# Moving key norms, the gated output, the second head's turn and two down-weight rotations inside one attention phase's hand-written engine orders

## The chip, the cores and the metric

The kernel runs on one core of a Trainium2 chip. It is one program with one launch. The metric is device time in microseconds (us), from the first to the last instruction and what lies around them; lower is better. Five engines run their own instruction lists side by side and meet only at semaphores: TensorE (PE: matmuls and transposes, which write PSUM), VectorE (DVE), ScalarE (ACT), GpSimd (POOL) and SyncE (SP, which issues the DMAs here).

## The reference, cut to what matters

Four stages work on x (16 x 112 x 512) with a context of 16 x 375 x 512: a causal cross attention, a feed forward stage with Hadamard transforms, a second cross attention with projected and normalized keys, and a last attention. The change lies in the first. That phase also prepares work for later stages: the keys and values of the third stage, which need only the context, and the turned and rotated weights of the second.

```python
x = x + tanh(g_xattn[0]) * L0_xattn(layernorm(x), ctx, ctx)      # first attention: q = layernorm(x), k = v = ctx
#   scores = q k^T / sqrt(32), causal mask, softmax, 16 heads of 32
x = x + tanh(g_ffn[0]) * L0_ffn(layernorm(x))                    # fwht, W_up and W_gate, silu, fwht, W_down
x = x + tanh(g_xattn[1]) * L1_xattn(layernorm(x), ctx)           # k = rms_norm(ctx @ Wk), v = ctx @ Wv, 4 heads of 128
x = x + tanh(g_ffn[1]) * L1_ffn(layernorm(x))
```

## The kernel before, in words

`phase_a` holds the first attention, and runs from about 6 us to about 688 us of the span. It works through B = 16 batches. Each has 8 pairs of heads (`PAIRS`, n = 0 to 7). PE, DVE and ACT each have a loop over b and n in which `if n == ...` lines set, by hand, at which place of that engine's list a step stands. An engine takes its list in this order, and a step that waits holds all that stand behind it. The names `cur`, `before` and `after` say that batch b, b - 1 or b + 1 exists.

The attention part of a pair: PE makes the scores of four heads (`scores`, for every second n), DVE masks and takes the maxima of a pair (`maximum(b, n)`), ACT takes the exponentials (`exps(b, n)`), PE turns the two heads' probabilities one after the other through one PSUM tile (`turn_probs(b, n, 0)`, then `(b, n, 1)`). After the first, ACT copies the tile out (`probs_copy`, semaphore `pT_first`); PE may fill the tile again only then. After the second, DVE copies (`pT_second`), and the first turn of the next pair waits for that. `weigh` multiplies by the context for a group of two pairs. After the batch `turn_back` turns the output, and DVE scales it (`gated`, semaphore `tmp_done`); POOL adds it to x (`residual`).

Beside this, in each batch:

- The context of the next batch is turned in three chunks (`turn_ctx(b + 1, c)`), and split in two float32r parts by ACT (`ctx_hi`) and DVE (`ctx_lo`). `turn_ctx(b + 1, 2)` writes the bank of the value projection, so PE waits there until ACT has copied the values of chunk 0 (`values_out(b, 0)`, semaphore `v_out`).
- The keys and values of the third stage are projected in three chunks, each in two halves of six matmuls (`project(b, "k" or "v", c, half)`). When the keys of a chunk stand in their bank, ACT squares them (`square_keys`), DVE sums the squares (`sum_keys`), POOL adds an epsilon and takes the power -1/2 (`key_norms`, tile `a_rk`), and DVE scales the keys (`scale_keys`, tile `a_kn`, semaphore `kn_done`). `project(b, "k", c + 1, 0)` writes the same bank, so PE waits for `kn_done`; `turn_keys` turns the scaled keys.
- Jobs for the second stage's weights (`run_job`, at n = 1, 3, 5, 7) turn gate, up and down weights through the bank `outp`, which many steps share: each waits for the reader of the use before (`free_out`). Down weights are first rotated on POOL (`rotate_down(b, 0 to 3)`, in batches with b % 4 of 0 or 1); the first job of b % 4 = 2 waits for all eight of these.
- DVE takes the moments of the next x (`moments(b + 1)`), POOL its deviation (`deviations`), DVE normalizes it (`normalize`, tile `a_xn`).

Of pair 1 to pair 3 the orders are, with the semaphore of a step's own waits left out. DVE, n = 1: `ctx_lo(b + 1, 0)`, `gated(b - 1)`, `probs_copy(b, 1)`, `moments(b + 1)`; n = 2: `maximum(b, 4)`, `sum_keys(b, 0)`, `probs_copy(b, 2)`, `maximum(b, 5)`, `normalize(b + 1)`; n = 3: `scale_keys(b, 0)`, `ctx_lo(b + 1, 1)`, `ctx_lo(b + 1, 2)`, `probs_copy(b, 3)`. ACT, n = 2: `square_keys(b, 0)`, `probs_copy(b, 2)`, `copy_out`, `exps(b, 4)`, `values_out(b, 0)`, `ctx_hi(b + 1, 1)`. POOL, per batch: `residual(b - 1)`, `deviations(b + 1)`, `key_norms(b, 0)` and what the diff shows.

Before the loop come the first turns and splits, and the split of the two projection weights into two parts (`weights_hi(0)`, `weights_hi(1)` on ACT, 2048 elements a row each; `weights_lo` on DVE).

## Time and profile before

| what | value |
|---|---|
| median of 3 runs | 2236.51 us (2234.78 to 2236.95) |
| profiled execution | 2239.38 us, its span 2237.7 us, mean granted TensorE clock 0.965 |
| busy over the span | PE 92%, DVE 59%, ACT 51%, POOL 30% |
| phase of the first attention | about 6 to 688 us |

The profiled execution stands 2.9 us above the median. Rows of the timeline give the start in us from the span's start, the duration in us, the engine, the line of the code, the tile written and the tiles read, how many instructions are merged, and in brackets the idle time of the engine ahead of the row and what ended it. A clock of 1.00 is TensorE's upper level of 2.4 GHz, 0.50 is the lower of 1.2 GHz.

### The profile page before, as it was taken

The page shows a single profiled execution, that of the slowest core. Times are in us where ns is not written, and L with a number is a line of the kernel's source. Part 1 is how long each engine was busy: PE and PEld are TensorE (multiplying, and loading weights), DVE is VectorE, ACT ScalarE, POOL GpSimd, SP SyncE. Part 2 cuts the span into 40 slices and gives each one's busy share as a digit, 9 for nine tenths or more (in the row PEclk, how much of TensorE's full clock was granted, in tenths as well). Part 3 has the DMA queues.
Part 4 walks back from the last instruction along what each step waited for, and adds up shares of the span by engine and source line. Part 5 has one row for each costly group of instructions (what it writes and reads, how often), then busy time and mean ns, then how long its engine had stood idle before and what let it go on. Part 6 is the DMA issues. An engine that isn't in the chain of part 4 may idle for free. (4 is left out here: it accounts for less than half of the span.)

```text
span 2237.7 us, 38580 instructions
## 1 busy us (share of the span) xinstructions
PE 2068.8 (92%) x13464; PEld 1704.7 (76%) x13464; DVE 1319.6 (59%) x2603; ACT 1148.4 (51%) x3025; POOL 664.6 (30%) x814
## 2 busy tenths in 40 slices
PE   5999999999998999999978996999999999689997
PEld 4767777777766888888857884888888888578884
DVE  5665656656654454465436554777777776466664
ACT  4555656556553333354323443766776676245542
POOL 1333523523522000000003442555555555012221
PEclk9999999999999999999989998999999999889997
DMA  4333534534328320010013344332223221221010
GB/s 147 122 115 123 150 90 133 183 90 139 113 70 301 103 73 18 1 66 29 1 67 107 114 125 133 102 105 94 74 92 104 96 80 37 78 73 47 26 34 26
DMA packets 167398, 205.96 MB, mean 92 GB/s; under 512 B 63680, under 2 KB 105664, under 8 KB 166752
## 3 DMA queue, kind: packets, MB, share of 16 engines
q1 hardware_dynamic: 167264, 204.15, 28.9%
q8 instruction: 87, 1.43, 0.3%
q14 instruction: 47, 0.39, 0.0%
HBM read 128.13 MB, written 75.99 MB: 91 GB/s over the span
## 5 line engine op out<-in xcount | busy, mean ns | idle before, releaser
L1730 POOL TENSOR_TENSOR c_probs<-c_probs,c_rsum 112x375 f32<-112x375 f32 x256 | 212.8, 834 | 231.5 <-DVE c_rsum L1840 225.6
L1836 DVE TENSOR_REDUCE c_nmax<-c_score 112x1 f32<-112x375 f32 x256 | 136.1, 532 | 97.3 <-PE c_score L1906 97.3
L1784 ACT ACTIVATE c_pT_hi<-c_turned 125x336 fp32r<-125x336 f32 x256 | 115.4, 451 | 108.1 <-PE c_turned L1914 108.1
L1225 ACT ACTIVATE b_silu<-b_gate,b_ug_scale 128x512 f32<-128x512 f32 (+1 forms) x64 | 40.7, 635 | 250.1 <-PE b_up L1331 250.0
L1282 DVE SCALAR_TENSOR_TENSOR b_hidden<-b_up,b_ug_scale,b_silu 128x512 f32<-128x512 f32 (+1 forms) x64 | 43.7, 683 | 204.2 <-ACT b_silu L1225 204.2
L919 PEld LDWEIGHTS a_turned<-keep_ident,a_probs 112*125 112x125 f32 x768 | 116.4, 194 | 52.1 <-issue 40.3
L919 PE MATMUL a_turned<-keep_ident,a_probs 112*125 112x112 f32 x768 | 136.5, 288 | 14.3 <-DVE a_pT L714 14.2
L1777 ACT ACTIVATE c_probs<-c_score,c_nmax 112x375 f32<-112x375 f32 x256 | 148.0, 578 | 0.0
L547 ACT ACTIVATE a_probs<-a_score,a_nmax 112x375 f32<-112x375 f32 x256 | 144.3, 573 | 5.8 <-DVE a_nmax L708 3.6
L1455 POOL TENSOR_TENSOR q_x_ve<-q_x_mv,keep_ln_eps 128x1 f32<-128x1 f32 x14 | 2.6, 189 | 444.7 <-DVE q_x_mv L1532 444.7
L1914 PEld LDWEIGHTS c_turned<-keep_ident,c_probs 112*125 112x125 f32 x768 | 121.7, 189 | 16.1 <-POOL c_probs L1730 7.2
L2141 ACT ACTIVATE f_probs<-f_score,f_nmax 112x112 f32<-112x112 f32 x256 | 87.1, 352 | 91.0 <-DVE f_nmax L2224 90.3
L2109 POOL TENSOR_TENSOR f_probs<-f_probs,f_rsum 112x448 f32<-112x448 f32 x64 | 60.1, 940 | 243.8 <-DVE f_rsum L2229 243.4
L1846 DVE TENSOR_TENSOR c_pT_lo<-c_turned,c_pT_hi 125x336 fp32r<-125x336 f32 x256 | 127.0, 496 | 4.6 <-ACT c_pT_hi L1784 2.8
L1914 PE MATMUL c_turned<-keep_ident,c_probs 112*125 112x112 f32 x768 | 123.4, 269 | 5.8 <-POOL c_probs L1730 5.3
L708 DVE TENSOR_REDUCE a_nmax<-a_score 112x2 f32<-112x750 f32 x128 | 120.1, 938 | 4.4
L1906 PE MATMUL c_score<-c_k_hi,c_q_hi 128*112 128x376 f32 x256 | 104.6, 409 | 16.4 <-DVE c_q_lo L1823 16.4
L705 DVE COPY_PREDICATED a_score<-keep_later,a_score 112x224 f32<-112x224 uint8 x128 | 49.9, 390 | 115.7 <-PE a_score L877 115.7
L714 DVE COPY a_pT<-a_turned 125x336 f32<-125x336 f32 x128 | 64.2, 502 | 79.1 <-PE a_turned L919 77.6
L466 POOL TENSOR_TENSOR a_ssq_eps<-a_ssq,keep_rms_eps 125x4 f32<-125x4 f32 x48 | 9.7, 201 | 331.6 <-DVE a_ssq L718 331.6
L555 ACT ACTIVATE a_pT<-a_turned 125x336 f32<-125x336 f32 x128 | 57.7, 451 | 78.5 <-PE a_turned L919 74.3
L1501 ACT ACTIVATE q_squares<-q_q_bank 128x512 f32<-128x512 f32 x56 | 33.4, 597 | 118.3 <-PE q_q_bank L1611 118.3
(306 smaller groups left out, 6033.2 us busy)
## 6 DMA issues: line engine op xcount, KB each, us to landing
q<-q_qT SPq DMA_DIRECT2D x14, 1024.0 KB
c_q_raw<-q SPq DMA_DIRECT2D x16, 896.0 KB
k<-ab_stage SPq DMA_DIRECT2D x16, 752.0 KB, 4.1
c_k_raw<-k SPq DMA_DIRECT2D x16, 752.0 KB
v<-ab_stage SPq DMA_DIRECT2D x48, 250.0 KB
c_v_raw<-v SPq DMA_DIRECT2D x16, 750.0 KB
ab_lead<-in_ctx_dram SPq DMA_DIRECT2D x16, 672.0 KB
wug<-a_ug_turned SPq DMA_DIRECT2D x32, 256.0 KB, 2.4
```

The lines of the kernel that those rows point to most:

```text
L547: last = act.activation(probs[:, n % RING, i, :], score[0:S, h % HPG, 0:T], ACT.Exp, bias=nmax[:, b % 2, h:h + 1], accum_out=sums[:, b % 2 ...
L708: dve.tensor_reduce(nmax[:, b % 2, 2 * n:2 * n + 2], score[0:S, pair, 0:T], axis=AX.X, op=ALU.max, negate=True).then_inc(max_done, 1)
L714: dve.tensor_copy(pT[:, g % 2, :, 2 * half + 1, :], turned[0:KP, 0:KC * S].rearrange("p (c s) -> p c s", c=KC)).then_inc(pT_second, 1)
L919: last = pe.transpose(turned[0:KP, c * S:(c + 1) * S], probs[:, n % RING, i, c * KP:(c + 1) * KP], ident[0:S, 0:S])
L1730: pool.tensor_tensor(probs[:, h % AHEAD, :], probs[:, h % AHEAD, :], rsum[:, p, h:h + 1].broadcast_to([S, T]), ALU.mult).then_inc(scaled, 1)
L1777: act.activation(probs[:, h % AHEAD, :], score[h % AHEAD][0:S, 0:T], ACT.Exp, bias=nmax[:, p, h:h + 1], accum_out=sums[:, p, h:h + 1]).the ...
L1784: act.activation(pT[0][:, g % 2, :, j, :], src, ACT.Copy).then_inc(pT_hi, 1)
L1836: dve.tensor_reduce(nmax[:, p, h:h + 1], score[h % AHEAD][0:S, 0:T], axis=AX.X, op=ALU.max, negate=True).then_inc(max_done, 1)
L1846: dve.tensor_tensor(pT[1][:, g % 2, :, j, :], src, f32(pT[0][:, g % 2, :, j, :]), ALU.subtract).then_inc(pT_split, 1)
L1906: last = pe.matmul(score[h % AHEAD][0:S, 0:TE], q[s][:, p, h, :], k[r][:, p, h // HPG, :], start=n == 0, stop=n == len(PASSES) - 1)
L1914: last = pe.transpose(turned[h % 2][0:KP, c * S:(c + 1) * S], probs[:, h % AHEAD, c * KP:(c + 1) * KP], ident[0:S, 0:S])
L2141: last = act.activation(probs[:, t % RING, j, :], score[0:S, SETS * (t % SETS) + a, half * S:(half + 1) * S], ACT.Exp, bias=nmax[:, t % RI ...
```

## The change

Only places in the lists change; every step does what it did, and waits for the same semaphores.

```diff
@@ POOL, per batch
                 key_norms(b, 0)
                 rotate_down(b, 0)
+                rotate_down(b, 1)
                 key_norms(b, 1)
-                rotate_down(b, 1)
+                rotate_down(b, 2)
                 if b:
                     output_deviations(b - 1)
+                rotate_down(b, 3)
                 key_norms(b, 2)
-                rotate_down(b, 2)
                 if b:
                     rotate_output(b - 1)
-                rotate_down(b, 3)
@@ ACT, before the loop and in it
             weights_hi(0)
             exps(0, 0)
+            exps(0, 1)
             weights_hi(1)
-            exps(0, 1)
...
-                    if n == 2 and cur:
-                        square_keys(b, 0)
...
                     if n == 1 and cur:
+                        square_keys(b, 0)
                         copy_job(b, 1)
@@ DVE, before the loop and in it
-            weights_lo(0)
             maximum(0, 0)
             maximum(0, 1)
+            weights_lo(0)
             weights_lo(1)
...
-                    if n == 3 and cur:
+                    if n == 2 and cur:
                         scale_keys(b, 0)
...
+                    if n == 1 and before:
+                        gated(b - 1)
                     if n == 1 and after:
                         ctx_lo(b + 1, 0)
-                    if n == 1 and before:
-                        gated(b - 1)
-                    if n == 2 and cur:
-                        sum_keys(b, 0)
...
+                    if n == 1 and cur:
+                        sum_keys(b, 0)
                     if n == 1 and after:
                         moments(b + 1)
@@ PE, in the loop
-                    if n == 2 and cur:
-                        project(b, "v", 0, 1)
...
-                    if n == 4 and cur:
-                        project(b, "v", 1, 0)
...
-                    if n == 6 and cur:
-                        project(b, "k", 2, 1)
...
                     if cur:
                         turn_probs(b, n, 1)
+                    if n == 2 and cur:
+                        project(b, "v", 0, 1)
+                    if n == 4 and cur:
+                        project(b, "v", 1, 0)
+                    if n == 6 and cur:
+                        project(b, "k", 2, 1)
```

`scale_keys(b, 0)` at n = 2 stands ahead of `maximum(b, 4)`. `square_keys(b, 0)` at n = 1 stands behind `exps(b, 3)` and ahead of `copy_job(b, 1)`. `sum_keys(b, 0)` at n = 1 stands behind `probs_copy(b, 1)` and ahead of `moments(b + 1)`.

## Rows read from the trace of the kernel before

**Rows 1.** Waits of PE, 0 to 700 us: total us, times, longest us.
```profile
PE a_keys L898 <- DVE a_kn L723: 24.7, 16, 1.9
PE a_turned L919 <- DVE a_pT L714: 14.2, 48, 0.7
...
PE a_outp L953 <- POOL a_down L504: 5.7, 4, 1.4
```

**Rows 2.** One stretch: length, busy us of five engines, granted clock, DMA share, GB/s.
```profile
204.00:210.00 6.00, 4.48 (x16) 3.79 (x17) 3.14 (x5) 1.87 (x6) 0.58 (x1) 0.72 0.38 107
```

**Rows 3.** Timeline, PE: key projection of chunk 1 starts, batches 3 and 4.
```profile
165.29 1.19 PE L898 MATMUL a_keys<-a_w_hi,a_kT_hi 128*125 128x512 f32 x4 [1.26 <-DVE a_kn L723]
...
205.52 1.97 PE L898 MATMUL a_keys<-a_w_hi,a_kT_hi 128*125 128x512 f32 x4 [1.85 <-DVE a_kn L723]
```

**Rows 4.** Timeline, PE in batch 3, from the job at n = 1 on.
```profile
156.48 0.66 PE L953 MATMUL a_outp<-keep_ident,a_down 128*128 128x128 f32 x4 [0.19 <-DVE ab_tmp L737]
...
159.68 0.78 PE L929 MATMUL a_outp<-a_pT,ab_lead 125*32 125x112 f32 x24
...
160.39 0.73 PE L898 MATMUL a_values<-a_w_lo,a_kT_hi 128*125 128x512 f32 x2
...
161.88 0.48 PE L919 MATMUL a_turned<-keep_ident,a_probs 112*125 112x112 f32 x3
...
163.05 0.55 PE L919 MATMUL a_turned<-keep_ident,a_probs 112*125 112x112 f32 x3 [0.26 <-DVE a_pT L714]
...
163.44 0.59 PE L855 MATMUL a_values<-keep_ident,ab_lead 125*128 125x125 f32 x4
```

**Rows 5.** Timeline, DVE, the same pairs of batch 3.
```profile
156.76 0.68 DVE L680 BATCH_NORM_STATS2 a_x_bn<-a_xin 112x6 f32<-112x512 f32 x1
...
159.29 0.40 DVE L705 COPY_PREDICATED a_score<-keep_later,a_score 112x224 f32<-112x224 uint8 x1 [1.64 <-PE a_score L877]
...
160.58 0.68 DVE L718 TENSOR_REDUCE a_ssq<-a_squares 125x4 f32<-125x512 f32 x1
...
162.39 0.51 DVE L714 COPY a_pT<-a_turned 125x336 f32<-125x336 f32 x1 [1.14 <-PE a_turned L919]
...
164.55 0.68 DVE L723 TENSOR_TENSOR a_kn<-a_keys,a_rk 125x512 f32<-125x512 f32 x1
```

**Rows 6.** Timeline, ACT, the same pairs.
```profile
157.18 0.60 ACT L593 ACTIVATE a_down_turned<-a_outp 128x512 f32<-128x512 f32 x1 [0.96 <-PE a_outp L953]
...
157.67 0.59 ACT L563 ACTIVATE a_squares<-a_keys 125x512 f32<-125x512 f32 x1
...
159.79 0.45 ACT L555 ACTIVATE a_pT<-a_turned 125x336 f32<-125x336 f32 x1 [1.53 <-PE a_turned L919]
...
160.69 0.57 ACT L547 ACTIVATE a_probs<-a_score,a_nmax 112x375 f32<-112x375 f32 x1
...
162.08 0.60 ACT L569 ACTIVATE ab_stage<-a_values 125x512 f32<-125x512 f32 x1 [0.17 <-PE a_values L898]
```

**Rows 7.** Timeline, POOL, the same pairs.
```profile
157.81 0.20 POOL L459 TENSOR_TENSOR a_x_ve<-a_x_mv,keep_ln_eps 112x1 f32<-112x1 f32 x1
...
158.09 0.56 POOL L461 TENSOR_TENSOR a_x_rstd<-a_x_ve,keep_neghalf 112x1 f32<-112x1 f32 x1
...
161.33 0.20 POOL L466 TENSOR_TENSOR a_ssq_eps<-a_ssq,keep_rms_eps 125x4 f32<-125x4 f32 x1 [2.69 <-DVE a_ssq L718]
...
161.61 1.01 POOL L468 TENSOR_TENSOR a_rk<-a_ssq_eps,keep_neghalf 125x4 f32<-125x4 f32 x1
```

**Rows 8.** Timeline, batch 4: a rotation on POOL beside the normalization on DVE.
```profile
202.23 2.35 POOL L504 TENSOR_TENSOR a_down<-a_down 128x1024 f32<-128x1024 f32 x1
...
203.74 1.13 DVE L688 TENSOR_SCALAR a_xn<-a_xin,a_x_mv,a_x_rstd 112x512 f32<-112x512 f32 x1
```

**Rows 9.** Timeline, the phase's start: first weight split on DVE, second scores on PE.
```profile
20.58 2.29 DVE L676 TENSOR_TENSOR a_w_lo<-a_down,a_w_hi 128x2048 fp32r<-128x2048 f32 x1 [1.12 <-ACT a_w_hi L528]
...
28.36 0.66 PE L877 MATMUL a_score<-a_kT_hi,a_qT_hi 32*112 32x376 f32 x4 [7.47 <-ACT a_probs L547]
```

## The prediction

> **What bounds the kernel now.** I read the busy shares first: PE is busy for 92% of the span, so PE sets the time, and what counts is time in which PE waits or runs at the lower clock. Next come PE's waits during the first attention. Three kinds concern this change [rows 1]. PE waits 16 times, once in each batch, for the scaled keys of chunk 0, 24.7 us in all. It waits 48 times, three times in each batch, for DVE's copy of the turned probabilities, 14.2 us. It waits 4 times for a rotation of the down weights, 5.7 us. Then the timeline, which shows a fixed pattern: the key wait is 1.26 us in the eight batches without rotations and about 1.85 us in the eight with them [rows 3]. Last the granted clock. In batch 4 it falls right after the key wait, and over 6 us its mean is 0.72, so 6 x 0.28 = 1.7 us of PE time goes [rows 2]. Such falls to 1.2 GHz stand behind nine of the sixteen key waits: seven of the eight long ones, two of the eight short ones. None stands behind the waits of 0.3 us. So the key wait costs 24.7 + 9 x 1.7 = 40 us, far more than its own row says.
>
> **The change part by part.** I take batch 3 as the pattern (no rotations, no fall) and move its rows.
>
> *Gated output ahead of the context split.* The job at n = 1 waited 0.19 us for `gated` [rows 4], in 11 of the batches (the other four wait for a rotation there, and batch 0 has no `gated`). `gated` gets ready some 0.6 us earlier, since the split ran ahead of it. The split starts 0.06 us later, and its reader, the value projection, comes 0.8 us after its end. Gain 11 x 0.19 = 2.1 us. PE is then at 159.49 where it was at 159.68.
>
> *Key norms of chunk 0.* ACT was free 0.96 us ahead of the copy at 157.18, so from 156.22 [rows 6]; the keys are in their bank at 156.0. Squares at 156.14 to 156.73, sum at 156.77 for 0.68. The moments of the next x, which stood at 156.76, now stand behind the sum and start at 157.37, so 0.61 later [rows 5]. POOL takes the deviation of the next x ahead of the key norms, so its two steps move from 157.81 to 158.42 and end at 159.26. Then the key norm: 0.28 from the first step to the second and 1.01 for that, which gives 160.53 [rows 7]. The keys are scaled from 160.57 to 161.25, where they were scaled from 164.55: 4 us earlier. The wait for `kn_done` is gone.
>
> What is queued behind that wait on DVE is `maximum(b, 4)`. It started at 159.29 and now can't start before 161.17, 1.9 us later. `exps(b, 4)` follows from 160.69 to 162.56, and `values_out(b, 0)` behind it from 162.08 to 163.7, ending at 164.3 [rows 5, 6]. For this copy waits `turn_ctx(b + 1, 2)` on PE, which ran at 163.44 and now starts at 164.37. DVE's copy of the second head of pair 2 comes behind the maxima at 162.43 and ends at 162.94, as late as before (162.90), so `turn_probs(b, 3, 0)` starts at 163.08 [rows 4, 5]. PE reaches it at about 162.55 and waits 0.5 us; it reaches the context turn at 163.47 and waits 0.9 us. The key projection starts about 0.48 us behind, at 164.85 instead of 165.29. So this part trades 0.26 + 1.26 us of waits for 0.5 + 0.9 us, and by 165.29 PE has won 0.44 us, of which 0.19 is the job's. Net gain of the key norms: 0.25 us a batch, 4 us in 16.
>
> That DVE can't take the maxima past a waiting `scale_keys` is read from the rows: in the trace the key norm is ready at 162.62, and `scale_keys` starts only at 164.55, behind work that is in front of it [rows 5, 7]. The Trainium skill ("TensorE: Matmul & The Clock Gate", section on the array's architectural detail) states that ACT and DVE are strict FIFO, and this trace agrees. Were it otherwise, the 1.4 us of new waits would vanish, and the change would be worth some 22 us more. This rule speaks against the new place of `scale_keys`.
>
> *In batches with rotations* the long wait had 0.59 us more, because the normalization of x took 1.13 us, beside a rotation of 2.35 us, and stood ahead of `scale_keys` [rows 8]. It now stands behind it, so this 0.59 goes, 8 x 0.59 = 4.7 us. Two rotations now run back to back from about 160.5 to 165.2. The normalization wants to start at 164.15, and ends at 165.5 at the latest if it must wait for the second. The context split behind it ends by 166.1, and `turn_keys` on PE wants it at 166.6. So nothing, with 0.5 us in hand.
>
> *Second head's turn ahead of the projection, n = 2, 4, 6.* Before, a projection half of 1.49 us (160.39 to 161.88) covered ACT's copy of the first head, and only a turn of 0.5 us covered DVE's copy of the second; hence the 48 waits [rows 1, 4]. Now `weigh` alone covers ACT's copy: PE's next step comes 0.71 us after `weigh` starts (159.68 to 160.39). ACT's copy starts 0.11 us after `weigh` starts and takes 0.45; with 0.15 us of handover, as between DVE's copy (ends 162.90) and PE (163.05), it is ready at 0.71 [rows 4 to 6]. So the cover is just enough. I take a wait of 0, with bounds 0 and 0.3 us each (the wait that the same tile costs today behind a short cover). The projection then covers DVE's copy, so the waits of n = 5 and 7 go: 2 x 0.29 = 0.57 us a batch. That of n = 3 is in the trade above. Batch 15 has nothing between the turns and waits longer there (up to 0.7 us [rows 1]); with no next x either, I estimate 2 us more for it. Sum: 16 x 0.57 + 2 = 11 us, bounds 11 and 11 - 48 x 0.3 = -3.
>
> *Rotations.* The last is done before `key_norms(b, 2)` instead of after `rotate_output`, over 30 us before the job that needs it. The four waits go: 5.7 us. The job doesn't meet the 0.19 either. Key norms of chunk 1 and 2 come up 10 us after the chunk before, and two rotations take 4.7, so neither is delayed.
>
> *Start.* The second scores waited 7.47 us for the exponentials, and DVE's maxima stood behind the first weight split of 2.29 us, which itself waited for ACT [rows 9]. Now the maxima start at 20.9, when the scores are there, and end at 23.6. Both exponentials end at 24.8, the second scores start at 24.9 instead of 28.36: 3.5 us. Both splits move back on DVE, the second ends at 29.0; then come the next maxima and the first copy of a second head, until 30.7. PE reaches its next wait for that at 31.0. So 3.5 us pass through, bounds 2 and 3.5.
>
> *Clock.* Each batch keeps about 1.4 us of waits in pair 3, in two pieces close together. That is nearest to the short class, with 1.26 us and a 0.26 us piece ahead of it, of which two in eight lost the clock. So I take four falls for nine: gain 5 x 1.7 = 8 us. Bounds: no fall (15 us) and a fall in each batch (a loss of 12 us).
>
> The sum: 2.1 + 4 + 4.7 + 11 + 5.7 + 3.5 = 31 us of waits, and 8 us of clock, 39 us. From the profiled execution's 2239.4 us this is 2200.5. That one was 2.9 us above the median, so against the median I put 2198.
>
> **The rivals.**
>
> (a) The clock decides otherwise. The waits shrink as worked out, but are close enough together to cost the clock in most batches: 2236.5 - 31 + 5 = 2211. For: they are 1.4 us within 1.9 us. Against: no piece is over 0.9 us. Or none falls at all, and the turn of the context waits less than I think: 2236.5 - 31 - 15 - 4 = 2186.
>
> (b) The waits only change their name: the 48 waits pass from DVE's to ACT's copy, 0.3 us each, and pair 3 gains nothing. Then there remain 2.1 + 4.7 + 5.7 + 3.5 = 16 us, and none to three of the clock falls go: 2219. For: the cover of `weigh` fits to within 0.05 us. Against: in the rows ACT is idle when the copy comes (1.53 us at n = 2).
>
> (c) Slower than before: `scale_keys(b, 0)` at its new place blocks DVE for longer than worked out, since POOL serves the residual and the next x's deviation first. Each us by which it starts after 160.57 goes in full through maxima, exponentials and the copy of the values to PE: 16 us a us. From 2.4 us on, the 39 us are spent; a single rotation (2.35 us) between would do it. At 3 us: 2198 + 48 = 2246. Against: the order puts no rotation ahead of `key_norms(b, 0)`, and POOL's steps repeat to within 0.1 us.
>
> (d) The change doesn't do what it says: another wait in pair 3 holds PE to the old time, and only the start and the rotations show, 9 us: 2227.
>
> **How the numbers follow.** The forecast of 2198 has 0.57, with its own range of 2191 to 2206. Rival (a) has 0.11 above and 0.12 below, (b) 0.11, (c) 0.04, (d) 0.05. The range for 8 in 10 is 2186 to 2212: it takes in both sides of (a) and leaves out (b), (c) and (d), 0.20 in all. A measurement of this kernel can tell about 0.2% (4.5 us) from no change. Faster by more than that: all but (c) and a little of (d), 0.94. Within it 0.02, slower 0.04.
>
> **What would show it.** In the changed profile: no wait of `a_keys` for `a_kn` in pair 3; in its place a wait of `a_values` L855 for ACT's `ab_stage` of about 0.9 us, 14 to 15 times, and of `a_turned` for `a_pT` of 0.5 us once a batch, no longer three times. `a_kn` of chunk 0 starts about 4 us ahead of the key projection and ends right before a mask. No wait for `a_down`. The second scores start near 25 us. Falls of the clock in about four batches. The prediction is wrong if `a_turned` waits for ACT's `a_pT` with over 0.1 us, if `a_kn` of chunk 0 starts more than 5 us after PE's job at n = 1, or if the falls are fewer than two or more than eight.

## The result, and the profile after

The changed kernel took 2182.72 us (median of 4 runs, 2182.15 to 2185.53). The kernel before, beside it on the same chip, took 2235.65 us (4 runs, 2234.47 to 2236.95). The ratio is 0.9766, with an interval of 0.9749 to 0.9783: faster by 52.9 us. The prediction was 2198.0 with a range of 2186 to 2212. The time fell 3.3 us below the range's lower end: the direction was right, the size too small by 15 us.

The profiled execution took 2183.04 us. First its page: span, busy time of each engine, and the granted TensorE clock in 40 slices.

```profile
span 2181.3 us, 38580 instructions
...
PE 2042.6 (94%) x13464; PEld 1691.5 (78%) x13464; DVE 1316.7 (60%) x2603; ACT 1139.9 (52%) x3025; POOL 666.3 (31%) x814
...
PEclk9999999999999999999979997999999999799997
```

PE is still the bound, now at 94%. The first twelve slices, some 650 us, hold the first attention, and none stands below 9. To see what of the time lies in that phase, I read the first and last start of the second stage's first matmul group, before and after (columns: duration ns min/median/max, then first and last start in us):

```profile
L1331 PE MATMUL b_gate<-ab_first,b_wu_hi x256: 274/386/794, 690.8 to 1023.1; 128*128 128x512 f32 x64, 128*128 128x256 f32 x64
```

```profile
L1330 PE MATMUL b_gate<-ab_first,b_wu_hi x256: 274/387/796, 635.8 to 968.6; 128*128 128x512 f32 x64, 128*128 128x256 f32 x64
```

The second stage starts 55.0 us earlier (690.8 to 635.8); the two profiled executions differ by 56.3. So all but about 1 us of the gain lies in the phase that was changed. In all kernels below, the profiled execution's time less that start is 1546 to 1549 us; so the start is a finer measure of one execution than the median of runs on different chips.

PE's waits in the first 640 us of after (total us, times, longest us):

```profile
PE a_values L854 <- ACT ab_stage L569: 11.6, 15, 0.8
PE a_turned L918 <- DVE a_pT L713: 9.6, 16, 1.0
...
PE a_score L876 <- ACT a_probs L547: 4.0, 1, 4.0
```

They stand against [rows 1] and the 7.5 us of [rows 9]. The 16 waits for `a_kn`, the 4 for `a_down` and the short ones of the jobs for `ab_tmp` are gone, and of the 48 for `a_pT` 16 are left. Now the timeline of pair 3 in batch 3, the trade that the prediction worked out (start us, us, engine, line, operation; in brackets the idle time before it and who ended it):

```profile
149.22 0.69 DVE L722 TENSOR_TENSOR a_kn<-a_keys,a_rk 125x512 f32<-125x512 f32 x1 [2.21 <-POOL a_rk L468]
149.83 0.39 DVE L704 COPY_PREDICATED a_score<-keep_later,a_score 112x224 f32<-112x224 uint8 x1
150.25 0.94 DVE L707 TENSOR_REDUCE a_nmax<-a_score 112x2 f32<-112x750 f32 x1
...
151.22 0.57 ACT L547 ACTIVATE a_probs<-a_score,a_nmax 112x375 f32<-112x375 f32 x1 [2.07 <-DVE a_nmax L707]
...
151.75 0.55 PE L918 MATMUL a_turned<-keep_ident,a_probs 112*125 112x112 f32 x3 [0.57 <-DVE a_pT L713]
...
152.33 0.59 ACT L569 ACTIVATE ab_stage<-a_values 125x512 f32<-125x512 f32 x1
...
153.07 0.62 PE L854 MATMUL a_values<-keep_ident,ab_lead 125*128 125x125 f32 x4 [0.77 <-ACT ab_stage L569]
```

This is the forecast chain: the scaled keys (L722) ahead of the mask (L704), the maxima late, the exponentials behind them, the copy of the values (L569) behind those, and PE waiting 0.57 and 0.77 us where 0.5 and 0.9 were predicted. The key projection behind it no longer waits for the keys. The section with this pair, from the scores at n = 2 to those at n = 4, got 0.22 us shorter (11.40 to 11.18), and 0.25 was worked out. So the mechanism was met, and the 15 us must lie elsewhere.

The granted clock is one place. Before, it fell nine times in this phase, as behind the key wait of batch 4 [rows 2]. In after, stretches of 2 us show a single fall, in batch 0 (columns: length, PE busy, granted clock, DMA share, GB/s). The low clock around the last wait of 6.4 us ahead of the second stage, which every kernel here has, isn't counted in either:

```profile
42.00:44.00 2.00, 2.00 (x8) 0.63 0.48 126
44.00:46.00 2.00, 2.00 (x10) 0.52 0.32 117
```

What the waits' rows don't contain is the other. A piece of work that comes back every two pairs shows it: the scores (L877 before, L876 after) at n = 4 and 6 of batch 3 and at n = 0 of batch 4. First before, then after:

```profile
169.87 0.43 PE L877 MATMUL a_score<-a_kT_hi,a_qT_hi 32*112 32x376 f32 x4
...
174.47 0.55 PE L919 MATMUL a_turned<-keep_ident,a_probs 112*125 112x112 f32 x3 [0.31 <-DVE a_pT L714]
...
178.94 0.44 PE L877 MATMUL a_score<-a_kT_hi,a_qT_hi 32*112 32x376 f32 x4
...
184.29 0.55 PE L919 MATMUL a_turned<-keep_ident,a_probs 112*125 112x112 f32 x3 [0.26 <-DVE a_pT L714]
...
188.76 0.43 PE L877 MATMUL a_score<-a_kT_hi,a_qT_hi 32*112 32x376 f32 x4
```

```profile
158.00 0.43 PE L876 MATMUL a_score<-a_kT_hi,a_qT_hi 32*112 32x376 f32 x4
...
166.52 0.44 PE L876 MATMUL a_score<-a_kT_hi,a_qT_hi 32*112 32x376 f32 x4
...
175.87 0.43 PE L876 MATMUL a_score<-a_kT_hi,a_qT_hi 32*112 32x376 f32 x4
```

The first section took 9.07 us and takes 8.52: 0.55 less, for a wait whose row says 0.31. The second took 9.82 and takes 9.35: 0.47 less, for a row of 0.26. The third, up to the scores at n = 2 of batch 4 (198.10 before, 184.80 after) and with a job's wait of 0.19 in it, took 9.34 and takes 8.93: 0.41 less. The clock is full in all of these. Each of these three waits was worth 0.21 to 0.24 us more than its row.

### The profile page after: what moved, and what is told of

Same layout as the page of the kernel before. It is cut to its first block and busy times, and to the rows that moved or that the text cites. A ratio compares the mean times of both kernels' runs of the same rounds, so it can differ in the third digit from the quotient of the medians.

```text
span 2181.3 us, 38580 instructions
## 1 busy us (share of the span) xinstructions
PE 2042.6 (94%) x13464; PEld 1691.5 (78%) x13464; DVE 1316.7 (60%) x2603; ACT 1139.9 (52%) x3025; POOL 666.3 (31%) x814
## 5 line engine op out<-in xcount | busy, mean ns | idle before, releaser
L918 PEld LDWEIGHTS a_turned<-keep_ident,a_probs 112*125 112x125 f32 x768 | 110.6, 189 | 47.0 <-issue 34.7
L1913 PEld LDWEIGHTS c_turned<-keep_ident,c_probs 112*125 112x125 f32 x768 | 121.8, 189 | 16.3 <-POOL c_probs L1729 7.4
L704 DVE COPY_PREDICATED a_score<-keep_later,a_score 112x224 f32<-112x224 uint8 x128 | 49.7, 388 | 82.0 <-PE a_score L876 82.0
L1342 PE MATMUL b_y<-b_wd_hi,b_hT_hi 128*128 128x512 f32 x224 | 87.8, 392 | 1.9 <-DVE b_hT_lo L1286 1.9
```

The costliest lines, as they stand in the source:

```text
L918: last = pe.transpose(turned[0:KP, c * S:(c + 1) * S], probs[:, n % RING, i, c * KP:(c + 1) * KP], ident[0:S, 0:S])
L1342: last = pe.matmul(y[b][:, :], hT[s][:, p, b * P:(b + 1) * P], wd[r][:, p, :], start=c == 0 and k == 0, stop=c == IC - 1 and k == len(PASS ...
L1913: last = pe.transpose(turned[h % 2][0:KP, c * S:(c + 1) * S], probs[:, h % AHEAD, c * KP:(c + 1) * KP], ident[0:S, 0:S])
```

## The experiments

Each kernel is compared with the kernel before on the same chip; it read 2236.26 us beside the first four, 2239.04 beside the next four and 2234.18 beside the last four. This table sums up the twelve. "Stage 2" is the start of the second stage in the profiled execution, "falls" the number of falls of the granted clock before it, counted as above; the first of the ten in e8 lasts twice as long as the others.

| kernel | median us | ratio to before (interval) | stage 2, us | falls |
|---|---|---|---|---|
| before | 2235.65 | 1 | 690.8 | 9 |
| after | 2182.72 | 0.9766 (0.9749 to 0.9783) | 635.8 | 1 |
| e1 turns back | 2201.63 | 0.9845 (0.9822 to 0.9868) | 653.6 | 0 |
| e2 norms back | 2189.86 | 0.9791 (0.9769 to 0.9812) | 638.6 | 2 |
| e3 rotations back | 2190.58 | 0.9794 (0.9772 to 0.9815) | 642.3 | 1 |
| e4 maxima first | 2168.92 | 0.9695 (0.9675 to 0.9716) | 621.6 | 0 |
| e5 gated back | 2183.06 | 0.9748 (0.9727 to 0.9770) | 635.2 | 0 |
| e6 start back | 2186.02 | 0.9763 (0.9743 to 0.9784) | 637.9 | 0 |
| e7 scale twice | 2198.35 | 0.9820 (0.9799 to 0.9841) | 651.9 | 5 |
| e8 scale thrice | 2219.77 | 0.9910 (0.9887 to 0.9932) | 670.7 | 10 |
| e9 turns alone | 2204.87 | 0.9869 (0.9851 to 0.9887) | 656.6 | 4 |
| e10 norms back, x late | 2160.71 | 0.9671 (0.9654 to 0.9687) | 612.9 | 0 |
| e11 maxima first, x late | 2160.52 | 0.9670 (0.9653 to 0.9687) | 612.2 | 0 |
| e12 norms alone | 2209.49 | 0.9886 (0.9869 to 0.9902) | 662.7 | 1 |

### What a wait costs: the turns back

Theory 1: a wait costs its row and about 0.24 us. Theory 2: the rows are right, and the extra gain is something else. The edit puts three projection halves ahead of the second head's turn again, in after:

```
+                    if n == 2 and cur:
+                        project(b, "v", 0, 1)
                     if n == 3 and after:
                         turn_ctx(b + 1, 2)
+                    if n == 4 and cur:
+                        project(b, "v", 1, 0)
...
+                    if n == 6 and cur:
+                        project(b, "k", 2, 1)
...
                         turn_probs(b, n, 1)
-                    (the same three projections)
```

> The changed kernel with one part undone: the three projection halves of n = 2, 4, 6 stand ahead of the second head's turn again. Two theories on why the change brought 53 us instead of 39. Theory 1: a wait of TensorE costs about 0.2 us more than its row says, since the row counts from the modelled end of the matmul before, while the next one could have started some 0.2 us ahead of that end. Then the two waits that come back in each batch (rows of 0.31 and 0.26 us, at n = 5 and n = 7) cost 0.24 + 0.31 + 0.21 + 0.26 = 1.0 us a batch, 16 us in all: 2199 us. Theory 2: a row is the whole price, and the surplus came from the clock alone: 16 x 0.57 = 9 us: 2192 us. Both expect 32 more waits of a_turned for DVE's a_pT with some 9 us in all.

The 48 waits are back:

```profile
PE a_turned L918 <- DVE a_pT L713: 19.5, 48, 1.0
```

Their rows are 9.9 us above after's, but the median rose by 18.9 us. The sections in its timeline show where:

```profile
159.88 0.43 PE L876 MATMUL a_score<-a_kT_hi,a_qT_hi 32*112 32x376 f32 x4
...
164.48 0.55 PE L918 MATMUL a_turned<-keep_ident,a_probs 112*125 112x112 f32 x3 [0.31 <-DVE a_pT L713]
...
168.96 0.43 PE L876 MATMUL a_score<-a_kT_hi,a_qT_hi 32*112 32x376 f32 x4
...
174.30 0.55 PE L918 MATMUL a_turned<-keep_ident,a_probs 112*125 112x112 f32 x3 [0.26 <-DVE a_pT L713]
...
178.81 0.43 PE L876 MATMUL a_score<-a_kT_hi,a_qT_hi 32*112 32x376 f32 x4
```

9.08 us against 8.52 (0.56 for a row of 0.31), 9.85 against 9.35 (0.50 for a row of 0.26). So 0.25 and 0.24 us stand on top, at the full clock. The other order of the projections isn't the reason: the section from n = 2 to n = 4 of the same batch, in which a projection moved too and the two waits kept their size, takes 11.17 us here and 11.18 in after. 32 more waits make 32 x 0.24 = 7.7 us, with the rows 17.6; the second stage starts 17.8 us later, and 19.5 at as many falls as after had. Of the 1.9 us between, 0.8 is the last pair of matmuls ahead of the second stage (L971), which runs at the low clock here (1.86 us against 1.02); 1.1 stay unassigned. Theory 1 stands, and theory 2, with the rows' 9.9, falls.

What the hidden part is can be read where PE's order is the same with a wait and without it. Two of the kernels below, e2 and e10, differ only in the place of the normalization. Batch 3, first with the key wait, then without:

```profile
151.75 0.62 PE L855 MATMUL a_values<-keep_ident,ab_lead 125*128 125x125 f32 x4
152.63 1.19 PE L898 MATMUL a_keys<-a_w_hi,a_kT_hi 128*125 128x512 f32 x4 [0.27 <-DVE a_kn L723]
```

```profile
145.26 0.62 PE L855 MATMUL a_values<-keep_ident,ab_lead 125*128 125x125 f32 x4
145.68 1.19 PE L898 MATMUL a_keys<-a_w_hi,a_kT_hi 128*125 128x512 f32 x4
```

Without a wait the second row starts 0.42 us after the first, which is 0.20 ahead of the first one's end; with the wait it starts 0.88 after. So the wait moved it by 0.46 us, and its row, counted from that end, says 0.27: what is missing is the overlap of the two rows. Where rows don't overlap, nothing is missing. The wait for ACT's copy of the values stands alone in batch 2 of e3, and is gone in batch 3 of e4:

```profile
113.79 0.48 PE L918 MATMUL a_turned<-keep_ident,a_probs 112*125 112x112 f32 x3
114.67 0.62 PE L854 MATMUL a_values<-keep_ident,ab_lead 125*128 125x125 f32 x4 [0.39 <-ACT ab_stage L569]
```

```profile
147.66 0.48 PE L918 MATMUL a_turned<-keep_ident,a_probs 112*125 112x112 f32 x3
148.17 0.62 PE L854 MATMUL a_values<-keep_ident,ab_lead 125*128 125x125 f32 x4
```

That is 0.88 us from start to start against 0.51: 0.37, for a row of 0.39. So the two waits of pair 3 together carry what one does: the section from n = 2 to n = 4 takes 11.18 us in after and 9.64 in e4, where both are gone, 1.54 for rows of 1.34. The ends of pipelined matmuls are modelled in the trace; whether the overlap is real or lies in those ends isn't shown, but the starts and the sections don't depend on it.

### Key norms back, and alone

```
-                        square_keys(b, 0)        (ACT, n = 1)
+                        square_keys(b, 0)        (ACT, n = 2, before copies)
-                    if n == 2 and cur:           (DVE)
+                    if n == 3 and cur:
                         scale_keys(b, 0)
-                        sum_keys(b, 0)           (DVE, n = 1)
+                        sum_keys(b, 0)           (DVE, n = 2, behind the maximum)
```

> The changed kernel with the key norms of chunk 0 at their old places (squares at n = 2 on ScalarE, sum at n = 2 and scaling at n = 3 on VectorE). The key wait comes back, about 1.5 us in one piece and 2.1 us beside rotations. Waits alone are worth 16 x 0.35 + 8 x 0.6 = 10 us: 2193 us. Clock theory: falls of the clock follow the length of idle time in one place, so about nine of the sixteen batches fall again, 8 more than in the changed kernel, 1.6 us each: 13 us more, 2206 us. Rival: the falls went for another reason (the phase in which the waits of 0.3 us went too), and the clock stays up: 2193 us with one or two falls.

The key wait is back, but it isn't the old one. Batches 3 and 4:

```profile
152.63 1.19 PE L898 MATMUL a_keys<-a_w_hi,a_kT_hi 128*125 128x512 f32 x4 [0.27 <-DVE a_kn L723]
...
191.42 1.87 PE L898 MATMUL a_keys<-a_w_hi,a_kT_hi 128*125 128x512 f32 x4 [2.08 <-DVE a_kn L723]
```

Against [rows 3], it shrank from 1.26 to 0.27 us where no rotation runs, and grew from 1.85 to 2.08 where one does. The median is 7.1 us above after's, below both figures that were expected (2193 and 2206), and the second stage starts 2.8 us later with one fall more; the median's own runs spread from 2185.6 to 2192.0, and the falls differ from one execution to the next. So moving the key norms is worth 3 to 7 us once the turns are moved. Little of that is in the waits: the section with pair 3 takes 10.18 us here against 11.18 in after where no rotation runs (batch 3), and 11.59 against 10.77 where one does (batch 5, without a fall). The other way round, in the kernel before, the key norms alone:

> The kernel before with one part alone: the key norms of chunk 0 at their new places. Both theories expect waits of 0.57 us for a_pT and 0.78 us for the copy of the values in pair 3 instead of 0.26 and 1.26 (1.85) us; with the 0.24 us that each wait costs on top, equal in number, that is 0.17 us in eight batches and 0.76 us in the others, 7.5 us. Clock theory 1 (the falls of the kernel before came from the one long wait, and two short ones don't bring them): eight falls fewer, 13 us more: 2216 us. Clock theory 2 (the falls went by where the batches come to lie in time, whichever part shortens them): the number of falls is anywhere from one to nine, 2216 to 2229 us, and differs between executions.

It took 2209.49 us, 24.7 below the kernel before beside it, and better than the 2216 expected. The waits for `a_kn` (24.7 us) went; `a_pT` rose to 16.3 us in 48, `ab_stage` waits of 8.0 us in 11 came, and one fall was left of nine.

### The turns alone

The kernel before with only the three projections behind the second turn. Theory A: the key wait shrinks by itself, since it came from PE's late second turn. Theory B: it is POOL's and stays.

> The kernel before with one part of the change alone: the three projection halves of n = 2, 4, 6 behind the second head's turn. Theory A (the turns freed the key wait too): the second turn of pair 2 is done some 1.7 us earlier, so VectorE's queue behind it (copy, maxima, normalization, key scaling) moves up, and the key wait shrinks by itself from 1.26 to about 0.3 us, and from 1.85 to about 0.9 us where a rotation stands beside the normalization. With all three waits for a_pT gone (rows of 0.83 us a batch, and 0.24 us more for each) this part alone is worth 16 x (0.83 + 0.72 + 0.95) = 40 us, and with some falls of the clock gone 2190 us. Theory B (as predicted; the parts are separate): 16 x 1.05 us for n = 5 and 7 and 0.5 us for n = 3, 25 us at most, and the key wait stays at 1.3 to 1.9 us: 2212 us.

2204.87 us, 29.3 below the kernel before beside it, in a change for which the prediction had 11, and between the 2190 of theory A and the 2212 of theory B. DVE, POOL and PE, in batches 3 and 4:

```profile
156.67 0.68 DVE L723 TENSOR_TENSOR a_kn<-a_keys,a_rk 125x512 f32<-125x512 f32 x1
...
193.57 2.36 DVE L688 TENSOR_SCALAR a_xn<-a_xin,a_x_mv,a_x_rstd 112x512 f32<-112x512 f32 x1
```

```profile
193.30 2.35 POOL L504 TENSOR_TENSOR a_down<-a_down 128x1024 f32<-128x1024 f32 x1
```

```profile
157.41 1.19 PE L898 MATMUL a_keys<-a_w_hi,a_kT_hi 128*125 128x512 f32 x4 [0.28 <-DVE a_kn L723]
...
196.58 1.39 PE L898 MATMUL a_keys<-a_w_hi,a_kT_hi 128*125 128x512 f32 x4 [2.08 <-DVE a_kn L723]
```

Where no rotation runs, theory A is right: DVE's queue was late because PE's turn for `a_pT` stood behind a projection half, and without that the scaled keys come 1.2 us earlier, 4.84 us after the scores at n = 2 (151.83) where it was 6.08 (158.47 to 164.55). In the other eight batches the normalization now starts right behind the start of the rotation (193.57 against 193.30) and takes 2.36 us where it took 1.13 [rows 8]; the key wait grows. This stands between the two theories, and it is what the prediction had not seen: the two moves overlap. Alone they give 29.3 and 24.7 us, 54.0 together; with the 3.8 and 6.5 us of start and rotations (below) that would be 64. The whole change gives 52.9. Part of the overlap is the clock: there were nine falls to lose, and the two alone already lose five and eight.

### Rotations, gated output and start back, one at a time

```
                 rotate_down(b, 0)
-                rotate_down(b, 1)
                 key_norms(b, 1)
+                rotate_down(b, 1)
...              (2 behind key_norms(b, 2), 3 behind rotate_output(b - 1))
```

> The changed kernel with the order of rotations and key norms on GpSimd as before. Four waits of the down job come back with rows of about 1.4 us. Theory 1 (0.2 us on top of each row): 4 x 1.65 = 6.6 us, 2189 us. Theory 2: 5.7 us, 2188.5 us; the two can't be told apart here. A second rotation no longer stands beside the normalization of x; if that mattered it would be faster than this, below 2186 us. If the long waits of the kernel before (1.85 us) came from the order of rotations and not from the place of the scaling, waits of pair 3 would grow by 0.6 us in eight batches: 2194 us.

2190.58 us, 7.9 more than after; the second stage starts 6.5 us later. `a_down` waits 6.8 us in 4 where 5.7 were predicted, `a_pT` 9.4 in 12 and `ab_stage` 10.2 in 15.

```
                     if n == 1 and after:
                         ctx_lo(b + 1, 0)
                     if n == 1 and before:
                         gated(b - 1)         (again behind the split)
```

> The changed kernel with the gated output behind the context split again. The wait of the job at n = 1 comes back with a row of 0.19 us in 15 batches. With 0.24 us on top of a row (as the run with the turns put back shows between like steps) that is 15 x 0.43 = 6.5 us: 2189 us. By the row alone: 3 us: 2185.5 us.

2183.06 us. Its before read 2239.04, 3.4 above the before of after; by the ratios it isn't slower than after. Both figures that were expected, 2185.5 and 2189, were missed. The second stage starts at 635.2 with no fall, against 635.8 with one. The 14 short waits of the jobs are back (0.18 to 0.19 us, 2.6 in all), but pair 3 hands the time back:

```profile
150.28 0.55 PE L918 MATMUL a_turned<-keep_ident,a_probs 112*125 112x112 f32 x3 [0.18 <-DVE a_pT L713]
```

The wait for `a_pT` is 0.18 instead of 0.57 us. The copy that PE waits for stands behind DVE's maxima, and these behind POOL's key norm, none of which depends on when PE ends its job. The job's wait of 0.18 has shortened it by 0.39, which is its row and the 0.21 that the row doesn't show. The sections say the same: 0.40 us more with the job (8.95 to 9.35), 0.40 less with pair 3 (11.18 to 10.78). So what PE wins at n = 1 it waits for at n = 3. This move is worth 1 us at most (635.2 and one fall of 1.65 against 635.8), and the 2.1 us of the prediction were a gain handed back two pairs later.

```
             exps(0, 0)
-            exps(0, 1)
             weights_hi(1)
+            exps(0, 1)
...
+            weights_lo(0)
             maximum(0, 0)
             maximum(0, 1)
-            weights_lo(0)
```

> The changed kernel with the first maxima behind the first weight split again. The second scores start 3.5 us later, and nothing else moves: 2186 us. The rest of the phase stands 3.5 us later in time; if the place in time decides about the clock, the number of falls after the waits of pair 3 may change with it (2186 to 2195 us), if the waits alone decide, it stays at one or two.

2186.02 us; the second stage starts 2.1 us later with a fall less, which at 1.65 us a fall makes 3.8. By the medians it is 3.3 us, by the ratios too small to tell. The trace says 3.5: the second scores wait 7.5 us instead of 4.0. The prediction's 3.5 holds.

### The price of a late scaling

Rival (c) rested on a price: each us by which `scale_keys(b, 0)` comes later costs 16 us. Two kernels add one and two more products of the same size into spare tiles ahead of it, which nothing reads:

```
+                for n in range(1 if c == 0 else 0):      (2 in the other)
+                    dve.tensor_tensor(spare[n][:, :]..., keys..., rk..., ALU.mult)
                 dve.tensor_tensor(kn[:, :]..., keys..., rk..., ALU.mult).then_inc(kn_done, 1)
```

> The changed kernel with one more operation on VectorE: ahead of the scaling of chunk 0's keys the same product is written once more, into a spare tile (its result isn't used). The maxima behind it start 0.6 us later. If what queues behind the scaling goes in full to TensorE, the wait for a_pT grows from 0.57 to 1.17 us and each batch by 0.6 us: 9.3 us, 2192 us. If falls of the clock go by the idle time in one place, some of these 1.95 us (in two pieces) bring them, three to eight, 1.6 us each: 2197 to 2205 us. If they don't, 2192 us.

> The same with two such products: the maxima start 1.2 us later, 15 x 1.2 + 0.5 = 18.5 us, 2201 us without falls of the clock. Idle time in pair 3 is then 2.55 us within 3 us, more than anywhere in the kernel before (2.1 us). If idle time in one place brings the falls, most batches fall: ten to fifteen, 2217 to 2226 us. If it is something else, 2201 to 2206 us.

They took 2198.35 and 2219.77 us, 15.6 and 37.1 above after (by the ratios 12 and 32). The second stage starts 16.1 and 34.9 us later, with 4 and 9 falls more. PE's wait for `a_pT` in pair 3 grew from 0.57 to 1.16 and 1.76 us in 15 batches (the last has none), which is 8.9 and 17.9 us. With 1.65 us a fall (1.7 by the granted clock; a section with one is 1.6 us longer, 13.16 against 11.59 in e2) the falls make 6.6 and 14.9, and the first fall of the second kernel, twice as long, some 1.5 more: 15.5 and 34.3 us, the measured shift to within 1 us. So the price holds for the waits, 15 us a us, and the clock comes on top and doubles it. Batch 3 of the first of them, PE's wait and then the granted clock:

```profile
154.36 0.55 PE L922 MATMUL a_turned<-keep_ident,a_probs 112*125 112x112 f32 x3 [1.16 <-DVE a_pT L714]
```

```profile
156.00:162.00 6.00, 6.00 (x24) 0.72 0.46 122
162.00:168.00 6.00, 6.00 (x62) 1.00 0.15 44
```

With 1.34 us of waits in pair 3 one batch of 15 lost the clock (the first, where they are 1.79), with 1.93 five (and the first, with 2.34, kept it), with about 2.5 ten. But a single wait of 2.08 to 2.10 us lost it in 2 of 8 batches in e2 and in 4 of 8 in e9, and before seven of the eight waits of 1.85 us did. So more idle time brings more falls, and it doesn't decide alone. What else does is open.

### Past the change: the maxima first, and the normalization late

If pair 3's waits come from the maxima standing behind `scale_keys`, the other order takes them away:

```
-                    if n == 2 and cur:
-                        scale_keys(b, 0)          (ahead of the maximum)
...
                             maximum(b + 1, n + 2 - PAIRS)
+                    if n == 2 and cur:
+                        scale_keys(b, 0)          (behind it)
```

> The changed kernel with one more move: scale_keys(b, 0) stands behind maximum(b, 4) at n = 2 instead of ahead of it. If both remaining waits of pair 3 (0.57 us for VectorE's copy, 0.78 us for ScalarE's copy of the values) come from the maxima that queue behind the scaling, both go. Theory 1 (0.2 us on top of each row): 15 x (0.57 + 0.78 + 0.4) = 26 us, with batch 0 (1.8 us and one fall) 29 us: 2154 us. Theory 2 (rows alone): 15 x 1.35 + 3.5 = 24 us: 2159 us. Rival: the copy of the values waits for the projection and not for the exponentials, and only the first wait goes: 2183 - 12 = 2171 us.

2168.92 us, 13.8 below after, where 24 to 29 were expected; the rival's 2171 is near only by chance, since both waits of pair 3 went. One new wait came, in the eight batches with rotations:

```profile
PE a_outp L906 <- DVE a_kT_lo L693: 8.8, 8, 1.5
```

```profile
182.24 4.74 POOL L504 TENSOR_TENSOR a_down<-a_down 128x1024 f32<-128x1024 f32 x2
...
184.61 2.66 DVE L687 TENSOR_SCALAR a_xn<-a_xin,a_x_mv,a_x_rstd 112x512 f32<-112x512 f32 x1
...
188.00 0.62 PE L906 MATMUL a_outp<-keep_ident,a_kn 125*128 125x125 f32 x4 [1.06 <-DVE a_kT_lo L693]
```

The two rotations end at 186.98, the first of them at about 184.6, and the normalization, 0.54 us long elsewhere, starts with the second and ends at 187.27. So the next step is to take the normalization past them: `normalize(b + 1)` from n = 2 to n = 3 on DVE, once with the key norms at their old places, once with the maxima first.

```
-                    if n == 2 and after:
+                    if n == 3 and after:
                         normalize(b + 1)
```

> The changed kernel without its move of the key norms, and with the normalization of the next x one pair later on VectorE (n = 3, behind the copy of the second head, instead of n = 2). If the waits of 2.1 us in batches with rotations come only from the normalization that two rotations hold up, and the 0.27 us of the other batches from its own 0.54 us, the key wait goes in all batches but the last: 19.5 - 0.9 us of rows and 15 x 0.24 us on top, 22 us, and the falls of the clock with it (5 us): 2190 - 27 = 2163 us. Rival: the key scaling comes up against the maxima of pair 5 and the key norm instead, and a wait of 0.3 us stays in each batch: 2171 us.

> The kernel with the scaling of the keys behind maximum(b, 4), and the normalization of the next x at n = 3. In the kernel without the second move TensorE waits in eight batches about 1.1 us at turn_keys(b, 0) for the context split, which stands behind a normalization of 2.66 us beside two rotations. If the rotations hold that normalization and nothing else, these waits go: 8.8 us of rows and 8 x 0.24 on top: 2158 us. Rival: another step of VectorE is held by the rotations at its place, and half of the gain comes: 2163 us.

2160.71 and 2160.52 us, 22 below after and 73 to 74 below the kernel before beside them: the best of all, and equal. Of the waits for `a_kn` and `a_pT` the first has two left in 16 batches, 0.9 us at the key projection of the last and 0.4 near the start, the second one of 0.8 near the start, and neither has a fall. In the second the same pieces of batch 4 read:

```profile
179.38 4.75 POOL L504 TENSOR_TENSOR a_down<-a_down 128x1024 f32<-128x1024 f32 x2
...
184.54 0.54 DVE L687 TENSOR_SCALAR a_xn<-a_xin,a_x_mv,a_x_rstd 112x512 f32<-112x512 f32 x1
```

The normalization comes after the rotations and takes 0.54 us. The first of the two kernels doesn't move the key norms at all. So this part of the change, for which DVE's order was rebuilt, wasn't needed: what held the keys up was the late second turn, and beside rotations the normalization.

## Why the prediction was right or wrong

**The terms.** From the waits' rows: before 54.0 us in 79 waits (for `a_kn`, `a_pT`, `a_down`, `ab_tmp` of the jobs, and the start), after 25.2 us in 32. That is 28.8 us, against 31 predicted for the waits. On top come some 10.7 us that no row shows: outside pair 3, 45 waits fewer at 0.22 us make 9.9; in pair 3 two waits a batch carried 0.24 us together before (11.40 us for the section, rows of 1.52, and 9.64 in e4 without waits) and carry 0.20 after, 0.8 us over all batches. Eight falls of the clock at 1.65 us are 13.2 us, where 8 were predicted. The sum is 52.7 of the 55.0 us; 2.3 us are not assigned.

**Pair 3: right.** The scaled keys come ahead of the mask, 0.57 and 0.77 us of waits stand where 0.5 and 0.9 were put, in 14 batches; the first has 1.01 and 0.78. The rule that DVE doesn't take the maxima past a waiting `scale_keys` held: with the two in the other order (e4) both waits are gone.

**The second turn: direction right, term mis-sized.** "So the cover is just enough. I take a wait of 0" was met. "So the waits of n = 5 and 7 go: 2 x 0.29 = 0.57 us a batch" was the failing term. It took the rows at face value; e1 shows 0.56 us where the row says 0.31, and the turns' part of the change is 18 to 19 us instead of 11. The same was left out for the jobs and the rotations. With the clock's term it is the error: some 11 us of hidden parts and 5 of clock.

**The clock: mis-sized.** "So I take four falls for nine." There was one. The 1.34 us of waits were nearest to the short class, as argued, but that class lost the clock less often than I took: 1 in 15, not 4. Fewer than two falls was one of the prediction's own signs of being wrong, and it came. A fall cost what the rows of before said, 1.6 to 1.7 us.

**The key norms: taken as if alone.** The prediction let each edit act on the kernel before and added the results. It gave the key norms the whole key wait, 1.26 or 1.85 us a batch. The turns alone already bring it to 0.28 where no rotation runs (e9), so there the norms' move trades 0.28 for 1.34 us (1.0 us lost by the sections), and pays only beside rotations (0.8 us won) and in the clock. As part of the whole it is worth 3 to 7 us (e2), alone 24.7 (e12).

**Gated output: wrong in kind.** "Gain 11 x 0.19 = 2.1 us" named no one who would be late next. The chain of pair 3 was late next, and took it back (e5). The prediction had both facts, since it worked out that pair 3 hangs on POOL's key norm; it didn't join them. (In the rows the job's wait is there in 10 batches, not 11: the last has no split ahead of `gated`.)

**Rotations and start: right.** 5.7 us predicted, 6.5 to 7.9 measured for the rotations (four waits, 6.8 us of rows and 0.2 hidden in each); 3.5 and 3.3 to 3.8 for the start. "So nothing, with 0.5 us in hand", for the normalization beside two rotations, held in after, where it takes 1.34 us. In e4 it starts earlier, takes 2.66 us and becomes the next wait.

**The rivals.** (a)'s lower side, at 2186, was the nearest in number; its reasons, no fall and 4 us less at the context's turn, were met only in part (one fall, 0.77 us instead of 0.9). (b), waits that pass to ACT's copy, didn't come: `a_turned` never waits for it. (c) didn't come; its price of 16 us a us was right for the waits and left out the clock: 1.19 us cost 35 us (e8), so, by an estimate from that run, some 1.3 us and not 2.4 would have spent the 39. (d) is out, since all parts show.

**The range** was too narrow at the bottom for one reason: it had bounds for the falls and for the cover, and none for what a removed wait is worth beyond its row. That alone came to 11 us.

## What to carry to other kernels

A wait's row isn't its price: where rows overlap without a wait, the overlap is lost too. Measure a repeated section between two like instructions, or the two starts around the wait, once with and once without it, before multiplying rows by counts. Where several waits hang on one queue, work out the moves together: a late turn on PE can be the cause of the wait that another edit is meant to cure, and a gain ahead of a chain that doesn't depend on it is handed back at that chain. Keep a long GpSimd operation away from the VectorE operation that it holds, here the normalization; by the start of the second stage its place in the order was worth 26 us with the key norms at their old places (e2 to e10) and 9 with the maxima first (e4 to e11).

## What the runs showed of the hardware

A rotation on POOL holds DVE's normalization to its end. It ended 0.28 to 0.29 us behind the end of the rotation in each case: 204.87 against 204.58 before [rows 8], 195.93 against 195.65 in e9, 187.27 against 186.98 in e4, for durations of 1.13, 2.36 and 2.66 us instead of 0.54. With two rotations back to back it is held by the one that runs when it starts, and not by both. In e4 it starts with the second; in e2 it starts within the first, and the second is the one that gives way (POOL, both rotations merged, then the second by itself, then DVE):

```profile
188.13 4.86 POOL L504 TENSOR_TENSOR a_down<-a_down 128x1024 f32<-128x1024 f32 x2
190.45 2.55 POOL L504 TENSOR_TENSOR a_down<-a_down 128x1024 f32<-128x1024 f32 x1
188.40 2.37 DVE L688 TENSOR_SCALAR a_xn<-a_xin,a_x_mv,a_x_rstd 112x512 f32<-112x512 f32 x1
```

The normalization ends at 190.77, 2.2 us ahead of the end of the two, and the second rotation takes 2.55 us instead of 2.35. The masks, maxima and key products that ran elsewhere in the same batches kept their durations (0.38 to 0.40, 0.94, and 0.68 to 0.69 us, also within a rotation). The Trainium skill ("SBUF — State Buffer", section "Who interferes with whom") states that DVE and GpSimd share a port pair as an exclusive lock, that `tensor_scalar` can take it, and that the one that comes second is blocked for the other's whole instruction. These durations agree, in both directions.

At the places read here where PE's rows overlap without a wait (by 0.20 us at 145.68 in e10), a wait costs 0.19 to 0.25 us beyond its row, whatever its length: 0.47 us for a row of 0.27 (10.18 against 9.71, batch 3 of e2 and e10), 2.29 for 2.10 (11.59 against 9.30, batch 5), 1.91 for 1.70 (10.84 in batch 2 of e3 against 8.93 in after), and the five sections above. The wait for ACT's copy of the values, at a place without overlap, costs its row (0.37 us for 0.39).

The number of falls of the clock isn't fixed for a kernel: the mean granted clock of four executions of after was 0.971, 0.971, 0.972 and 0.968, and the one at 0.968 took 3 us longer than the others.
